# Attention jobs of a routed transformer layer: a result copy split by PSUM bank, an earlier reciprocal, and a register bound for the last stores

## The chip, the core and the metric

One NeuronCore of a Trainium2 chip. Its engines run side by side, each through its own queue, and meet only at semaphores: TensorE (PE in the profile; PEld is its weight loads), VectorE (DVE), ScalarE (ACT), GpSimd (POOL) and SyncE (SP, which issues DMAs). The metric is the device time of one execution in microseconds; lower is better.

## The reference

A gated cross-attention block and then a routed feed-forward block, float32 throughout. Two batches of 512 tokens of width 256, a context of 1024 keys, 16 heads of 64, 8 experts:

```python
# attention: q from the normalised x, k and v from the context, masked softmax
qh = heads_split(q @ Wq); kh = heads_split(k @ Wk); vh = heads_split(v @ Wv)
dots = jnp.einsum('bhid,bhjd->bhij', qh, kh) * scale
dots = jnp.where(mask[:, None, :, :], mask_value, dots)
out = einsum('bhij,bhjd->bhid', softmax(dots), vh) ... @ Wo + bo
...
# experts: each token takes the one expert with the largest gate
idx = jnp.argmax(softmax(xf @ Wg + bg), axis=-1)
h = gelu(xf @ W1[e] + b1[e]); y = h @ W2[e] + b2[e]; out = y[idx]
...
x = x + tanh(g_xattn) * attention(layernorm(x), ctx, ctx, mask)
x = x + tanh(g_ffn) * experts(layernorm(x))
```

With the inputs given, the mask leaves a window of 160 keys per batch, so the kernel takes its windowed path (`rest(False)` on all engines).

## The kernel before, in words

The order on each engine is written out by hand; semaphores tie the engines together, and nothing reorders the work afterwards. One batch of attention is `attend_window(b, ...)`, which exists once for each engine. It runs over 8 **jobs** (`JOBS`), each with two **units** (u = 2·job and 2·job + 1). A unit is one pair of heads for two tiles of 128 query rows, so it has four score blocks of 128 × 160. A unit goes through the engines so:

- PE, `scores(u)` (L1751): eight matmul records into `s_bank[u % 2]`.
- DVE, `window_max(b, u)` (L1307): for each tile, for each head, one custom instruction that scales, masks and takes a running minimum (of the negated scores). Four instructions per unit; "a pair of minima" is the two heads of one tile. `negm_ready` counts them.
- ACT, `window_exp` (L827): four exponentials per unit with their row sums, after two minima each. `probs_ready` counts units.
- DVE, `window_sum(b, u)` (L1318): the reciprocal of the row sums, into `r_col`.
- POOL, `normalise_window` (L645, L647): multiplies the unit's probabilities by the reciprocal, first the wide part (128 of the 160 keys), then the left-over 32 keys, into `left_probs`. `pn_ready` counts both.
- PE, `transposes(job)`: four transposes for the job's first unit, four for its second (L1768, into `t_bank`), and two **left transposes** (L1779) of the left-over keys. The left transposes write the upper half of PSUM bank 7, which is also the right half of `o_bank` (`o_bank[:, 1]`); its lower half holds one half of the result of the job before.
- DVE and ACT copy the transposes out of PSUM: `job_pT_rest` (L1328, a wide one of 512 columns and a left one of 256) and `job_pT_wide` (L836).
- PE, `values(job)` (L1790 left keys, L1797 wide keys), into both halves of `o_bank`.
- DVE, `job_o(b, job)` (L1333): copies the job's result out of `o_bank` to `oT`.

In the loop of job j, PE stands at scores of the next job, values of the job before, transposes of this one. In the same loop DVE does: minima of unit 2j+2 (four), reciprocal of unit 2j+1, minima of unit 2j+3 (four), copy of the result of job j−1, reciprocal of unit 2j+2, the two copies of this job's transposes, and then what hangs on `also(job)`: in the second batch, after jobs 4, 5 and 6, the normalisation of one chunk of 128 sorted rows for the experts (`norm_chunk`, L1241). POOL in the second batch also sends scatter DMAs after units 1, 3 and 5 (`sort_first_batch`, L609).

What PE waits for in `transposes(job)`: the left transposes wait for `first.o_dve`, that is for the whole copy of the result of job j−1. `values(job)` waits for the same count.

After both batches come output projections, routing, and the experts, in two rounds of eight chunks (L2000, L2011, L2022 on PE). DVE adds each chunk's result into its rows (`take_y`, L1256), and POOL sends them to their places in the output by an indirect DMA, `put_out(g, p)` (L624), 16 in all. Each has a bound on the row index, `bounds_check=T - 1`, given as a number; in the built program a register move stands ahead of each of these DMAs and carries the wait for `y_taken`. Ahead of the last of them POOL loads a flag (`over_any`, L704).

Of the kernel before, what the change touches and what calls it, by code (L numbers as in the profile page):

```python
# [97 lines left out]
def flamingo_kernel(nc, x, ctx_in, mask, g_xattn, g_ffn, wq, wk, wv, wo, bo, wg, bg, w1, b1, w2, b2, out):  # L98
# [13 lines left out]
    T = B * N  # L112
# [24 lines left out]
    with ExitStack() as stack:  # L137
# [191 lines left out]
        empty_ready = sem("empty_ready")  # L329
        s_out = sem("s_out")  # L330
        left_zero = sem("left_zero")

        head_rows = [slice(r * DH, (r + 1) * DH) for r in range(2)]

# [224 lines left out]
        def _(pool):  # L559
# [58 lines left out]
                    .then_inc(experts[g].b2_added, 1)  # L618

            out_rows = out.rearrange("b n d -> (b n) d")  # L620

            def put_out(g, p):
                pool.wait_ge(experts[g].y_taken, p + 1)
                nc.gpsimd.indirect_dma_start(out=out_rows, in_=srow[g][:, p, 0:D], in_offset=None,  # L624
                                             out_offset=bass.IndirectOffsetOnAxis(
                                                 ap=srow[g][:, p, TOKEN:RW].bitcast(I32), axis=0),
                                             bounds_check=T - 1, oob_is_err=False).then_inc(s_out, 16)

            def normalise(S, g, keys, also):
                for u in range(PER):  # L630
# [46 lines left out]
            def rest(later_too):  # L677

                if later_too:
                    pool.wait_ge(visits_listed, 1)  # L680
                for b in range(B):
                    if later_too:
                        normalise(first, b * PER, CK, nothing if b == 0 else sort_first_batch)
                    else:
                        normalise_window(b, nothing if b == 0 else sort_first_batch)
                    if later_too:
                        later_visits(b)
                    if b == 0:
                        add_bo()
                        pool.wait_ge(s_b2, 16)  # L690
                        nc.gpsimd.tensor_scalar(b2_sb[:], b2_sb[:], gate[:, 1:2], None, ALU.mult).then_inc(b2_ready, 1)

                for e in range(E):
                    add_b2(0, e, e)
                for r in range(1, len(ROUTED)):
                    pool.wait_ge(place_ready, r + 1)
                    for q in range(QT // 2):
                        scatter(r, q)
                for e in range(E):
                    put_out(0, e)  # L700
                for e in range(E - 1):
                    put_out(1, e)
                pool.wait_ge(over_ready, 1)
                any_over = pool.value_load(over_any[0:1, 0:1], min_val=0, max_val=1)  # L704
                put_out(1, E - 1)
                with pool.If(any_over > 0):
                    pool.wait_ge(over_listed, 1)
                    used = pool.value_load(over_used[0:1, 0:1], min_val=0, max_val=NV)
                    for k in range(NV):
                        with pool.If(used > k):  # L710
                            pool.reg_mov(chunk_expert, pool.value_load(over_code[0:1, k:k + 1], min_val=0, max_val=E - 1))
                            e = pool.snap(chunk_expert, min_val=0, max_val=E - 1)
                            pool.wait_ge(experts[2].sxn_ready, k + 1)
                            nc.gpsimd.tensor_tensor(srow[2][:, k, 0:D], srow[2][:, k, 0:D],
                                                    b2_sb[:, bass.ds(e, 1), :].rearrange("p e d -> p (e d)"), ALU.add)\
                                .then_inc(experts[2].b2_added, 1)
                            put_out(2, k)
                            pool.wait_ge(s_out, 16 * (B * E + k + 1))
                        with pool.Else():
                            pool.nop()  # L720
                with pool.Else():
                    pool.nop()
# [303 lines left out]
        def _(dve):  # L1026
# [266 lines left out]
                dve.wait_ge(S.o_ready, g + (u + 1))  # L1293
                nc.vector.tensor_copy(*o_dst(slot, u)).then_inc(S.o_dve, 1)

            def window_max(b, u):

                m, j = unit_of(u)
                if u >= PB:

                    dve.wait_ge(first.ptrans_ready, 3 * (b * JOBS + (u - PB) // 2) + 3)
                dve.wait_ge(first.scores_ready, b * PER + (u + 1))
                for i in range(2):
                    q = 2 * j + i
                    for h in range(2):

# [23 lines left out]
            def job_o(b, job):  # L1330
                quad, j = job // 2, job % 2
                dve.wait_ge(first.o_ready, b * JOBS + job + 1)
                nc.vector.tensor_copy(oT[:, b, 2 * quad:2 * quad + 2, j * HALF:(j + 1) * HALF],  # L1333
                                      o_bank[:, :, 0:HALF]).then_inc(first.o_dve, 1)

            def attend_window(b, w, fill, also):

# [22 lines left out]
                nc.vector.tensor_copy(*left_v_dst(3)).then_inc(first.v_dve, 1)  # L1360
                for job in range(JOBS):
                    if job + 1 < JOBS:
                        window_max(b, 2 * job + 2)
                    if job >= 1:
                        window_sum(b, 2 * job + 1)
                    if job + 1 < JOBS:
                        window_max(b, 2 * job + 3)
                    else:
                        fill(0)
# [213 lines left out]
        def _(pe):  # L1583
# [155 lines left out]
            def attend_window(b, fill, also):  # L1739
# [16 lines left out]
                def transposes(job):  # L1756
# [13 lines left out]
                        last.then_inc(first.ptrans_ready, 1)  # L1770
                    if job >= 1:

                        pe.wait_ge(first.o_dve, b * JOBS + job)
                    else:
                        pe.wait_ge(first.v_act, b * 2 + 2)
                        pe.wait_ge(first.v_dve, b * 2 + 2)
# [431 lines left out]
```

## Time and profile before

| | |
|---|---|
| median of 3 runs | 203.22 us (203.05 to 204.3) |
| the profiled execution, its own time | 204.05 us |
| its span | 202.2 us |
| PE busy | 191.9 us (95%) |
| DVE busy | 123.4 us (61%) |
| ACT busy | 106.4 us (53%) |
| POOL busy | 89.7 us (44%) |
| mean granted TensorE clock | 0.988 of full speed |

The span is what the profiler saw from the first instruction to the last; the execution's own time has 1.85 us more around it. The shares are means over stages that differ much: the attention jobs of the two batches lie at 38 to 76 us and at 112 to 146 us, the experts' second round and the last stores at 178 us to the end. The end of a matmul record is modelled by the profiler, so PE can look busy while its queue waits; the weight loads (PEld) show where it stood.

### The profile page before, as it was taken

The page shows a single profiled execution, that of the slowest core. Times are in us where ns is not written, and L with a number is a line of the kernel's source. Part 1 is how long each engine was busy: PE and PEld are TensorE (multiplying, and loading weights), DVE is VectorE, ACT ScalarE, POOL GpSimd, SP SyncE. Part 2 cuts the span into 40 slices and gives each one's busy share as a digit, 9 for nine tenths or more (in the row PEclk, how much of TensorE's full clock was granted, in tenths as well). Part 3 has the DMA queues.
Part 4 walks back from the last instruction along what each step waited for, and adds up shares of the span by engine and source line. Part 5 has one row for each costly group of instructions (what it writes and reads, how often), then busy time and mean ns, then how long its engine had stood idle before and what let it go on. Part 6 is the DMA issues. An engine that isn't in the chain of part 4 may idle for free.

```text
span 202.2 us, 3980 instructions
## 1 busy us (share of the span) xinstructions
PE 191.9 (95%) x1252; PEld 140.7 (70%) x1252; DVE 123.4 (61%) x537; ACT 106.4 (53%) x380; POOL 89.7 (44%) x129
## 2 busy tenths in 40 slices
PE   7999999899999999999999799999999999999950
PEld 6984364667775544888876566775788889989940
DVE  2479665999986421253448999997824547265520
ACT  3243537899998112211528699998441254445510
POOL 7000004367767992000002899677920014775451
PEclk9999999999999999999999999999999999999995
DMA  5997017999999980570000110600000001353011
GB/s 146 342 367 245 0 30 231 347 275 321 300 307 252 211 293 6 159 256 0 3 2 0 45 36 29 212 3 0 0 3 2 0 0 64 112 159 107 33 40 40
DMA packets 22322, 25.16 MB, mean 124 GB/s; under 512 B 1988, under 2 KB 20878, under 8 KB 22161
## 3 DMA queue, kind: packets, MB, share of 16 engines
q1 hardware_dynamic: 19536, 21.83, 36.8%
q0 software_dynamic: 1152, 2.12, 3.1%
q10 hardware_dynamic: 1600, 0.84, 1.5%
q8 instruction: 13, 0.21, 0.5%
q14 instruction: 21, 0.16, 0.3%
HBM read 14.14 MB, written 11.68 MB: 128 GB/s over the span
## 4 chain that ended last, share of the span: by engine, by line
PE 83%; DVE 9%; issue 2%; ACT 2%; POOL 1%; POOLq 0%; DVEq 0%
PE s_bank L1711 14%; PE o_bank L1656 14%; PE s_bank L2011 7%; PE o_bank L1797 7%; PE s_bank L1751 6%; PE o_bank L2022 6%; PE t_bank L1768 6%; PE o_bank L1790 3%; DVE probs L1307 3%; PE s_bank L1590 3%; DVE pT L1328 2%; PE s_bank L1822 2%; PE s_bank L1621 2%; PE t_bank L1805 2%; PE t_bank L1682 2%
## 5 line engine op out<-in xcount | busy, mean ns | idle before, releaser
L645 POOL TENSOR_TENSOR probs<-probs,r_col 128x512 f32<-128x512 f32 x32 | 33.4, 1042 | 76.4 <-DVE r_col L1318 76.1
L827 ACT ACTIVATE probs<-probs,negm_run 128x160 f32<-128x160 f32 x128 | 53.0, 416 | 5.3 <-DVE negm_run L1307 5.2
L1307 DVE CUSTOM_DVE_ANT_0 probs<-s_bank,maskneg 128x160 f32<-128x160 f32 x128 | 33.2, 318 | 3.9 <-PE s_bank L1751 3.6
L1711 PE MATMUL s_bank<-xnT,wq_sb 128*128 128x512 f32 x64 | 28.8, 597 | 0.0
L1656 PE MATMUL o_bank<-wo_sb,oT 128*128 128x256 f32 x128 | 28.7, 380 | 0.0
L1656 PEld LDWEIGHTS o_bank<-wo_sb,oT 128*128 128x128 f32 x128 | 23.9, 190 | 3.5 <-issue 0.5
L827 ACT ACTIVATION_READ_ACCUMULATOR probs<-probs,negm_run 128x1 f32 x128 | 24.0, 187 | 0.0
L1751 PE MATMUL s_bank<-k_sb,q_sb 64*128 64x160 f32 x256 | 22.1, 310 | 0.2 <-DVE negm_run L1307 0.2
L1751 PEld LDWEIGHTS s_bank<-k_sb,q_sb 64*128 64x128 f32 x256 | 17.9, 186 | 4.3 <-issue 3.5
L1711 PEld LDWEIGHTS s_bank<-xnT,wq_sb 128*128 128x128 f32 x64 | 11.7, 190 | 13.0 <-issue 12.8
L624 POOL DMA_INDIRECT out_dram<-oT x16 | 16.0, 1002 | 9.3 <-DVE oT L1256 7.2
L1768 PE MATMUL t_bank<-ident,probs 128*128 128x128 f32 x128 | 19.1, 285 | 0.2 <-POOL probs L645 0.2
L1768 PEld LDWEIGHTS t_bank<-ident,probs 128*128 128x128 f32 x128 | 13.5, 140 | 7.8 <-issue 5.7
L1797 PE MATMUL o_bank<-pT,v_sb 128*64 128x256 f32 x128 | 17.5, 393 | 0.0
L609 POOL DMA_INDIRECT sorted_rows<-rows,place x8 | 8.1, 1006 | 21.2 <-DVE place L1198 19.8
L2011 PE MATMUL s_bank<-k_sb,q_sb 128*128 128x128 f32 x128 | 17.2, 277 | 0.2 <-ACT k_sb L925 0.2
L2011 PEld LDWEIGHTS s_bank<-k_sb,q_sb 128*128 128x128 f32 x128 | 15.7, 192 | 1.0 <-ACT k_sb L925 0.5
L2022 PE MATMUL o_bank<-oT,k_sb 128*128 128x256 f32 x64 | 16.4, 383 | 0.0
L1256 DVE SCALAR_TENSOR_TENSOR oT<-o_bank,gate,oT 128x256 f32<-128x256 f32 x16 | 7.6, 483 | 12.5 <-PE o_bank L2022 12.5
L787 ACT COPY q_sb<-s_bank 128x512 f32<-128x512 f32 x10 | 5.8, 586 | 17.2 <-PE s_bank L1711 14.7
L934 ACT ACTIVATE k_sb<-s_bank,b1T 128x128 f32<-128x128 f32 x32 | 10.0, 365 | 8.8 <-PE s_bank L2011 8.4
L1230 DVE SCALAR_TENSOR_TENSOR rows<-o_bank,gate,rows 128x256 f32<-128x256 f32 x8 | 3.9, 483 | 16.1 <-PE o_bank L1656 16.1
(169 smaller groups left out, 301.1 us busy)
## 6 DMA issues: line engine op xcount, KB each, us to landing
sorted_rows<-empty_row SPq DMA_DIRECT2D x8, 1040.0 KB, 15.2
oT<-in_L_ffn_W_dram SPq DMA_DIRECT2D x1, 2048.0 KB, 19.2
q_sb<-in_L_ffn_W_dram SPq DMA_DIRECT2D x1, 2048.0 KB, 8.4
oT<-sorted_rows SPq DMA_DIRECT2D x1, 1040.0 KB, 5.0
oT<-sorted_rows SPq DMA_DIRECT2D x8, 130.0 KB, 2.3
wq_sb<-in_L_xattn_Wq_dram SPq DMA_DIRECT2D x2, 512.0 KB, 8.3
mask_sb<-in_mask_BxSxS_bk_dram SPq DMA_DIRECT2D x2, 512.0 KB, 9.1
wv_sb<-in_L_xattn_Wv_dram SPq DMA_DIRECT2D x1, 1024.0 KB, 10.8
```

The source lines that it names most:

```text
L624: nc.gpsimd.indirect_dma_start(out=out_rows, in_=srow[g][:, p, 0:D], in_offset=None, out_offset=bass.IndirectOffsetOnAxis(ap=srow[g][:, p, ...
L645: nc.gpsimd.tensor_tensor(window_wide(u), window_wide(u), r.rearrange("p i h -> p (i h)") .unsqueeze(2).broadcast_to([P, 4, WIDE]), ALU.mu ...
L827: last = nc.scalar.activation(window_part(u, i, h), window_part(u, i, h), ACT.Exp, bias=negm_run[at], scale=-1.0, accum_out=l_run[at])
L934: last = nc.scalar.activation(hT[:, p % 2, at], hT_bank(p)[:, at], ACT.Gelu, bias=bias(ic))
L1307: nc.vector.tensor_tensor_reduce(window_part(u, i, h), s_bank[u % 2][:, h, i * CK:i * CK + WK], maskneg[:, q, 0:WK], -SCALE, LARGEST, ALU. ...
L1656: last = nc.tensor.matmul(bank[6 + tt % 2][:, 0:D], oT[:, b, m, q * P:(q + 1) * P], wo_sb[:, m, :], start=(m == 0), stop=(m == M - 1))
L1711: last = nc.tensor.matmul(bank[m % 4], wq_sb[:, c, m * P:(m + 1) * P], xnT[:, c, b * N:(b + 1) * N], start=(c == 0), stop=(c == DC - 1))
L1751: last = nc.tensor.matmul(s_bank[u % 2][:, h, i * CK:i * CK + WK], q_sb[head_rows[h], b, m, q * P:(q + 1) * P], k_sb[head_rows[h], m, 0:WK ...
L1768: last = nc.tensor.transpose(bank[4 + a][:, h * HALF + i * P:h * HALF + (i + 1) * P], window_wide(u)[:, 2 * i + h, :], ident[:])
L1797: last = nc.tensor.matmul(o_bank[head_rows[h], a, 0:HALF], v_sb[:, 0, at * DH:(at + 1) * DH], wide_pT[:, a, h, :], start=False, stop=True)
L2011: last = nc.tensor.matmul(hT_bank(e)[:, ic * P:(ic + 1) * P], w1_sb[:, e, c, ic * P:(ic + 1) * P], sxT[:, e % 2, c * P:(c + 1) * P], start ...
L2022: last = nc.tensor.matmul(bank[6 + p % 2][:, 0:D], hT[:, p % 2, ic * P:(ic + 1) * P], weights(ic), start=(ic == 0), stop=(ic == IC - 1))
```

## The change

Four edits:

1. `job_o` copies the result by banks: two copies of 256 columns in place of one of 512, the right half (bank 7) first. The right half has a semaphore of its own, `o_right`; the second copy increments `o_dve`. The left transposes of the next job wait for `o_right` alone. `values` still waits for `o_dve`.
2. In DVE's loop the reciprocal of unit 2j+1 moves ahead of the second pair of minima of unit 2j+2. It stood behind it.
3. The bound of the output DMAs sits in a register that is written once at the start; the DMA itself now carries the wait for `y_taken`.
4. POOL loads the flag `over_any` after the fourth store of the second round. It was loaded after the seventh.

```diff
+        o_right = sem("o_right")
...
+            last_row = pool.alloc_register("pool_last_row")
+            pool.reg_mov(last_row, T - 1)
 
             def put_out(g, p):
                 pool.wait_ge(experts[g].y_taken, p + 1)
...
-                                             bounds_check=T - 1, oob_is_err=False).then_inc(s_out, 16)
+                                             bounds_check=last_row, oob_is_err=False).then_inc(s_out, 16)
...
-                for e in range(E - 1):
+                for e in range(E // 2):
                     put_out(1, e)
                 pool.wait_ge(over_ready, 1)
                 any_over = pool.value_load(over_any[0:1, 0:1], min_val=0, max_val=1)
-                put_out(1, E - 1)
+                for e in range(E // 2, E):
+                    put_out(1, e)
...
-            def window_max(b, u):
+            def window_max(b, u, tiles=(0, 1)):
 
                 m, j = unit_of(u)
-                if u >= PB:
-
-                    dve.wait_ge(first.ptrans_ready, 3 * (b * JOBS + (u - PB) // 2) + 3)
-                dve.wait_ge(first.scores_ready, b * PER + (u + 1))
-                for i in range(2):
+                if tiles[0] == 0:
+                    if u >= PB:
+
+                        dve.wait_ge(first.ptrans_ready, 3 * (b * JOBS + (u - PB) // 2) + 3)
+                    dve.wait_ge(first.scores_ready, b * PER + (u + 1))
+                for i in tiles:
...
                 dve.wait_ge(first.o_ready, b * JOBS + job + 1)
-                nc.vector.tensor_copy(oT[:, b, 2 * quad:2 * quad + 2, j * HALF:(j + 1) * HALF],
-                                      o_bank[:, :, 0:HALF]).then_inc(first.o_dve, 1)
+                for a, taken in ((1, o_right), (0, first.o_dve)):
+                    nc.vector.tensor_copy(oT[:, b, 2 * quad + a, j * HALF:(j + 1) * HALF],
+                                          o_bank[:, a, 0:HALF]).then_inc(taken, 1)
...
                     if job + 1 < JOBS:
-                        window_max(b, 2 * job + 2)
+                        window_max(b, 2 * job + 2, (0,))
                     if job >= 1:
                         window_sum(b, 2 * job + 1)
                     if job + 1 < JOBS:
+                        window_max(b, 2 * job + 2, (1,))
                         window_max(b, 2 * job + 3)
...
                     if job >= 1:
 
-                        pe.wait_ge(first.o_dve, b * JOBS + job)
+                        pe.wait_ge(o_right, b * JOBS + job)
```

How the rows stand on DVE in the loop of job 2, at the reciprocal. Before (each ISA pair is one minimum and the read of its result; the reciprocal is that of unit 5, between the minima of units 6 and 7):

```order
L1307 ISA probs,negm_run<-s_bank,maskneg 128x160 [waits scores_ready_first,ptrans_ready_first]
L1307 ISA negm_run 128x1
L1307 ISA probs,negm_run<-s_bank,maskneg 128x160
L1307 ISA negm_run 128x1
L1307 ISA probs,negm_run<-s_bank,maskneg 128x160
L1307 ISA negm_run 128x1
L1307 ISA probs,negm_run<-s_bank,maskneg 128x160
L1307 ISA negm_run 128x1
L1318 RECIPROCAL r_col<-l_run 128x4 [waits pn_ready_first,probs_ready_first]
L1307 ISA probs,negm_run<-s_bank,maskneg 128x160 [waits scores_ready_first,ptrans_ready_first]
```

Now:

```order
L1312 ISA probs,negm_run<-s_bank,maskneg 128x160 [waits scores_ready_first,ptrans_ready_first]
L1312 ISA negm_run 128x1
L1312 ISA probs,negm_run<-s_bank,maskneg 128x160
L1312 ISA negm_run 128x1
L1323 RECIPROCAL r_col<-l_run 128x4 [waits pn_ready_first,probs_ready_first]
L1312 ISA probs,negm_run<-s_bank,maskneg 128x160
L1312 ISA negm_run 128x1
L1312 ISA probs,negm_run<-s_bank,maskneg 128x160
L1312 ISA negm_run 128x1
L1312 ISA probs,negm_run<-s_bank,maskneg 128x160 [waits scores_ready_first,ptrans_ready_first]
```

The reciprocal stands two minima earlier, with the same waits; the third and fourth minimum are now behind those waits.

DVE again, the end of the same loop. Before:

```order
L1307 ISA negm_run 128x1
L1333 COPY oT<-o_bank 128x2x256 [waits o_ready_first]
L1318 RECIPROCAL r_col<-l_run 128x4 [waits pn_ready_first,probs_ready_first]
L1328 COPY pT<-t_bank 128x512 [waits o_ready_first,ptrans_ready_first]
L1328 COPY pT<-o_bank 128x256 [waits o_ready_first,ptrans_ready_first]
```

Now:

```order
L1312 ISA negm_run 128x1
L1339 COPY oT<-o_bank 128x256 [waits o_ready_first]
L1339 COPY oT<-o_bank 128x256
L1323 RECIPROCAL r_col<-l_run 128x4 [waits pn_ready_first,probs_ready_first]
L1333 COPY pT<-t_bank 128x512 [waits o_ready_first,ptrans_ready_first]
L1333 COPY pT<-o_bank 128x256 [waits o_ready_first,ptrans_ready_first]
```

One copy of two banks has become two copies of one bank. The rest keeps its order.

POOL, the stores at the end of the program (register moves are not listed). Before:

```order
L624 DMA out_dram<-oT 1024x256 [waits y_taken_first] x8
L624 DMA out_dram<-oT 1024x256 [waits y_taken_second] x7
L704 TENSOR_LOAD over_any [waits over_ready]
L704 ISA x2
L624 DMA out_dram<-oT 1024x256 [waits y_taken_second]
```

Now:

```order
L627 DMA out_dram<-oT 1024x256 [waits y_taken_first] x8
L627 DMA out_dram<-oT 1024x256 [waits y_taken_second] x4
L707 TENSOR_LOAD over_any [waits over_ready]
L707 ISA x2
L627 DMA out_dram<-oT 1024x256 [waits y_taken_second] x4
```

The load of the flag stands three stores earlier. PE's and ACT's queues hold the same instructions in the same order as before; on PE only the semaphore of the left transposes differs.

## Rows read from the trace of the kernel before

**Rows 1.** The chain of waits from 44 to 64 us, its shares by line.

```profile
by line: PE t_bank L1768 28.9%; PE s_bank L1751 27.1%; PE o_bank L1797 25.4%; PE o_bank L1790 10.8%; PE o_bank L1779 5.5%; PE s_bank L1711 4.3%
```

**Rows 2.** Timeline of weight loads: start us, us, engine, line, instruction, idle before.

```profile
49.63 0.42 PEld L1768 LDWEIGHTS t_bank<-ident,probs 128*128 128x128 f32 x4 [0.39 <-issue]
50.20 0.42 PEld L1768 LDWEIGHTS t_bank<-ident,probs 128*128 128x128 f32 x4
50.63 0.20 PEld L1779 LDWEIGHTS o_bank<-ident,pT 128*128 128x128 f32 x2
51.00 1.12 PEld L1751 LDWEIGHTS s_bank<-k_sb,q_sb 64*128 64x128 f32 x16 [0.17 <-issue]
55.11 1.12 PEld L1751 LDWEIGHTS s_bank<-k_sb,q_sb 64*128 64x128 f32 x16 [0.17 <-issue]
...
68.41 0.85 PEld L1768 LDWEIGHTS t_bank<-ident,probs 128*128 128x128 f32 x8 [0.39 <-issue]
69.27 0.21 PEld L1779 LDWEIGHTS o_bank<-ident,pT 128*128 128x128 f32 x2
```

**Rows 3.** Timeline of POOL, first batch and second batch.

```profile
49.10 1.04 POOL L645 TENSOR_TENSOR probs<-probs,r_col 128x512 f32<-128x512 f32 x1 [1.06 <-DVE r_col L1318]
...
120.51 0.41 POOL L647 TENSOR_TENSOR pT<-probs,r_col 128x128 f32<-128x128 f32 x1
121.03 1.04 POOL L645 TENSOR_TENSOR probs<-probs,r_col 128x512 f32<-128x512 f32 x1
```

**Rows 4.** Timeline of DVE, one loop in the first batch.

```profile
47.87 0.32 DVE L1307 CUSTOM_DVE_ANT_0 probs<-s_bank,maskneg 128x160 f32<-128x160 f32 x1 [0.40 <-PE s_bank L1751]
...
48.85 0.17 DVE L1318 RECIPROCAL r_col<-l_run 128x4 f32<-128x4 f32 x1
...
49.89 0.69 DVE L1333 COPY oT<-o_bank 128x512 f32<-128x512 f32 x1
...
50.49 0.17 DVE L1318 RECIPROCAL r_col<-l_run 128x4 f32<-128x4 f32 x1
```

**Rows 5.** Timeline of ACT, in job 1 and in a later job.

```profile
40.09 0.19 ACT L827 ACTIVATION_READ_ACCUMULATOR probs<-probs,negm_run 128x1 f32 x1
...
51.70 0.19 ACT L827 ACTIVATION_READ_ACCUMULATOR probs<-probs,negm_run 128x1 f32 x1
...
52.58 0.43 ACT L827 ACTIVATE probs<-probs,negm_run 128x160 f32<-128x160 f32 x1 [0.23 <-DVE negm_run L1307]
```

**Rows 6.** Timeline of the second batch, late jobs: DVE, and one weight load.

```profile
131.30 0.42 DVE L1328 COPY pT<-o_bank 128x256 f32<-128x256 f32 x1
131.63 0.44 DVE L1241 TENSOR_SCALAR wk_sb<-oT 128x256 f32<-128x256 f32 x1
132.12 0.32 DVE L1307 CUSTOM_DVE_ANT_0 probs<-s_bank,maskneg 128x160 f32<-128x160 f32 x1
...
139.98 0.30 PEld L1790 LDWEIGHTS o_bank<-pT,v_sb 64*128 64x128 f32 x4 [0.36 <-DVE pT L1328]
```

**Rows 7.** Timeline of DVE and POOL, a scatter's release and the last two stores.

```profile
165.48 0.17 DVE L1198 CAST place<-place_f 128x2 int32<-128x2 f32 x1
165.92 1.01 POOL L609 DMA_INDIRECT sorted_rows<-rows,place  x1 [17.71 <-DVE place L1198]
167.24 0.96 POOL L609 DMA_INDIRECT sorted_rows<-rows,place  x1 [0.30 <-issue]
...
194.25 0.48 DVE L1256 SCALAR_TENSOR_TENSOR oT<-o_bank,gate,oT 128x256 f32<-128x256 f32 x1 [1.27 <-PE o_bank L2022]
195.23 0.48 DVE L1256 SCALAR_TENSOR_TENSOR oT<-o_bank,gate,oT 128x256 f32<-128x256 f32 x1 [0.50 <-PE o_bank L2022]
195.52 0.98 POOL L624 DMA_INDIRECT out_dram<-oT  x1 [0.77 <-DVE oT L1256]
196.81 0.99 POOL L624 DMA_INDIRECT out_dram<-oT  x1 [0.30 <-issue]
```

## The prediction, made before the changed kernel was run

> **What bounds the kernel now.** I read the chain of waits first. Between 44 and 64 us, five jobs of the first batch, it lies on PE alone [rows 1]. That looks like an engine at its limit, but the end of a matmul record is modelled, so I went on to the weight loads, which show where PE's queue really stood. One job lasts 4.11 us, from the scores at 51.00 to those at 55.11 [rows 2]. In such a job the four transposes of the first unit load from 49.63, those of the second only from 50.20, after 0.15 us of nothing (49.63 + 0.42 = 50.05), and the left transposes at 50.63: 1.00 us after the first. In job 6, where projections stand between the jobs and everything has long been ready, the same ten transposes run through: 68.41 to 69.27 is 0.86 us [rows 2]. So each tight job holds 0.14 us in which PE waits, and 3.97 us are its own work.
>
> Who makes it wait? For the second unit's transposes it is POOL. Its wide multiplication runs from 49.10 to 50.14, and the load at 50.20 follows [rows 3]. POOL itself waited 1.06 us for DVE's reciprocal, which starts at 48.85, behind four minima that began at 47.87 [rows 4]; those waited for PE's scores. This is a ring: scores, four minima, reciprocal, POOL, transposes, scores. A second ring ends at the same moment: the copy of the result ends at 49.89 + 0.69 = 50.58 [rows 4], and the left transposes that wait for it load at 50.63. Taking away one of them alone would leave most of the 0.14 us. The change takes both.
>
> At the end of the program the bound is PE, then DVE, then POOL's stores. The last results are taken by 194.73 and 195.71 (starts 194.25 and 195.23 plus 0.48), and the last two stores start at 195.52 and 196.81 [rows 7].
>
> **The reciprocal earlier.** Four minima take 48.85 - 47.87 = 0.98 us, two take 0.49. The reciprocal starts 0.49 us earlier, POOL ends at 49.65 in place of 50.14, and the second unit's transposes could load at their natural 50.06. That leaves 0.4 us to spare. What is queued behind the reciprocal's wait now are the third and fourth minimum and, through them, ACT. The wait is for ACT's row sums of the unit before: their last read ends at 51.70 + 0.19 = 51.89 [rows 5], while the reciprocal would stand at 51.97 + 0.49 = 52.46. In a tight job it costs nothing. In job 1 it does: the sums end at 40.28 [rows 5] and the reciprocal would stand at about 40.15, so DVE waits some 0.15 to 0.2 us, once in each batch. Job 1 is not a tight one, and the result's copy, which is now shorter, makes up for it. I take nothing for job 1 (bounds: 0.03 gained, 0.1 lost).
>
> **The copy by banks.** A copy of 512 columns holds DVE 0.60 us (49.89 to the reciprocal at 50.49 [rows 4]), one of 256 columns 0.33 us (131.30 to 131.63 [rows 6]). So two of them take 0.66 us: 0.06 us more a job. The lower bound is nothing more; the upper is two full durations of 0.42, 0.24 us more. I take 0.06, which is read from a copy out of the same bank. The right half is ready at 49.89 + 0.42 = 50.31 in place of 50.58; the left transposes' natural place is 49.63 + 0.86 = 50.49. So this wait goes too, with 0.13 us to spare. The second copy has `values` of the next job as its waiter, over 1 us later on PE, so it costs nothing there.
>
> The Trainium skill, in VectorE: DVE Perf Modes, section on the TRN2 errata, speaks against the split: it gives a copy from PSUM to SBUF a fixed 120 cycles beside one cycle for each element. By it, as an estimate at 0.96 GHz, the second copy costs 0.125 us a job, twice the difference of the rows, and the second batch below would gain about 0.2 us less (0.065 three times).
>
> **What is late next.** PE's own 3.97 us. DVE's loop without an expert chunk is shorter: with a chunk it has 0.14 us to spare at 4.11 (the chunk starts at 131.63, holds DVE 0.44 - 0.09 = 0.35, and the next minimum comes at 132.12 [rows 6]), so 3.97 us with a chunk and 3.62 us without, and 4.03 and 3.68 after the split. ACT is idle 0.23 us a job [rows 5], so it needs 3.88.
>
> **First batch.** Five jobs have the wait (their transposes start at 45.52, 49.63, 53.74, 57.84 and 61.95): 5 x 0.14 = 0.70 us. Behind them PE runs projections without a break, so the gain is kept.
>
> **Second batch.** Five jobs again show the gap, but other engines stand close. In job 2 POOL, which also sends scatters here, is nearly full: unit 4's left part ends at 120.92 and unit 5 starts at 121.03 [rows 3]. It can start 0.1 us earlier at most: 0.09 us gained. Job 3 gains the full 0.14. From then on DVE decides, since the next loops carry the chunks: 4.11 - 4.03 = 0.08 us for each of two, and the last DVE stretch, up to the load at 139.98 that waits for the left copy [rows 6], is 0.06 us longer for the split. Sum: 0.09 + 0.14 + 0.16 - 0.06 = 0.33 us. The copy of the last job ends up to 0.06 us later with the first projection behind it; I take off 0.03. So 0.30 us. With the upper bound of the split (0.24 us) it would be 0.23 - 0.20 - 0.24, about 0.2 us lost.
>
> **The stores.** When a store has to wait for its result it starts 195.52 - 194.73 = 0.79 us after the result is taken; between lies the register move that carries the wait. The scatters carry their wait themselves: the place is there at 165.65, and the scatter starts at 165.92, 0.27 us later [rows 7]. The difference is 0.52 us. Back to back the distance is the same with and without the move (0.30 us idle between two scatters and between the last two stores [rows 7]), so nothing is gained where POOL is busy anyway. At the end: the last store but one starts at 194.73 + 0.28 = 195.01 in place of 195.52; the last follows 0.98 + 0.30 later, at 196.29, and its own result is ready by 195.71 + 0.28 = 195.99. So the end comes 0.52 us earlier; I write 0.5. The lower bound is 0, if the bound's register, which no scatter has, is what takes the time; below nothing there is no reason, since an instruction goes. The flag's load moves to where POOL idles 1 us between stores; the last two stores already stand at the back-to-back distance with it between them, so moving it gives nothing.
>
> **The sum.** 0.70 + 0.30 + 0.5 = 1.5 us. The profiled execution took 204.05 us, with a span of 202.2; it becomes 202.55, or 0.73% less. On the median of 203.22 us that is 201.7 us.
>
> **Rivals.**
> - The stores gain nothing, because reading the bound from a register is what takes the time. For it: no row shows a POOL DMA with a register that was not just written. Against: the move is the one thing that the scatter lacks and that also holds the wait. 203.2 - 1.0 = 202.2 us. Chance 0.15.
> - The loop gains nothing: PE's pieces need the 4.11 us in this order, and the 0.14 us appear again as a drain elsewhere, or DVE's dearer copy (0.24 us) takes them. Against it stand the 0.86 us of job 6. 203.2 - 0.5 = 202.7 us. Chance 0.10.
> - Slower: the reciprocal now blocks the minima. The ring is reciprocal, third and fourth minimum, ACT's six exponentials after them, row sums, the next such reciprocal. It decides as soon as ACT's sums come more than 0.57 us later than now relative to the minima (51.89 against 52.46). If the 0.17 us of job 1 came in each of the 12 later jobs: 2.0 us lost, 0.5 gained, 204.7 us. Against it: ACT has 0.23 us idle in a job. Chance 0.03.
> - More than I forecast: the 0.17 us of idle ahead of each job's scores [rows 2] is not the change of shape that it seems to be, but one more wait that goes. 10 x 0.17 us more: 200.0 us. It is there at the same length wherever scores follow left transposes, even where nothing is late. Chance 0.06.
> - The change does not do what it says, and all stays at 203.2 us. The queues show that it is built as written. Chance 0.02.
>
> **How the numbers follow.** The forecast has 0.64. Its own range is 201.2 to 202.3: the second batch between -0.2 and +0.4, the runs themselves spread by some tenths. With the first two rivals the range reaches to 203.0, and to 200.9 below for the larger gain. A measurement of this kernel can tell about 1% from no change, 2.0 us. Under 201.2 us lie the fourth rival and the lower end of the forecast: 0.15. Over 205.2 us lies hardly even the slower rival: 0.03. The rest, 0.82, is within 1%.
>
> **What the profile after would show.** Right: the distance from scores to scores 3.97 us in the first batch; second-unit transposes loading without a gap behind the first; POOL starting the odd unit about 0.75 us after the first minimum in place of 1.23; in the second batch 4.03 us where chunks are; the last store but one 0.28 us after its result. Wrong: a scores distance still at 4.11; a DVE wait on ACT at the reciprocal in every job; two result copies that hold DVE over 0.75 us together; a store 0.8 us after its result with no move ahead of it. What would make the whole wrong is a wait on PE that the modelled ends hide, since then the 0.14 us are not there to be had.

## The result, and the profile after

The changed kernel takes 202.31 us (median of 12 runs, 201.52 to 202.91) beside 203.66 us (median of 12 runs, 202.51 to 204.3) for the kernel before on the same chip. The ratio is 0.994, with a 95% interval of 0.9924 to 0.9956: 0.9 to 1.5 us were gained. (The forecast stood on the median of 3 runs on record then, 203.22 us.) The profiled execution took 201.97 us, with a span of 200.2 us, beside 204.05 and 202.2.

Timeline of the weight loads of the changed kernel, one loop of the first batch; it answers to [rows 2]:

```profile
46.31 1.12 PEld L1758 LDWEIGHTS s_bank<-k_sb,q_sb 64*128 64x128 f32 x16 [0.17 <-issue]
47.37 0.33 PEld L1797 LDWEIGHTS o_bank<-pT,v_sb 64*128 64x128 f32 x4
48.03 0.63 PEld L1804 LDWEIGHTS o_bank<-pT,v_sb 128*64 128x64 f32 x8 [0.33 <-issue]
49.05 0.86 PEld L1775 LDWEIGHTS t_bank<-ident,probs 128*128 128x128 f32 x8 [0.39 <-issue]
49.88 0.25 PEld L1786 LDWEIGHTS o_bank<-ident,pT 128*128 128x128 f32 x2
50.29 1.12 PEld L1758 LDWEIGHTS s_bank<-k_sb,q_sb 64*128 64x128 f32 x16 [0.17 <-issue]
```

The eight wide transposes are now one row: nothing stands between the first unit's and the second's. The left ones load 0.83 us after the first wide one, in place of 1.00. From scores to scores it is 50.29 - 46.31 = 3.98 us, where [rows 2] has 4.11.

POOL in the same loop answers to [rows 3], and DVE (the reads of the minima's accumulators left out) to [rows 4]:

```profile
48.03 1.04 POOL L648 TENSOR_TENSOR probs<-probs,r_col 128x512 f32<-128x512 f32 x1 [0.38 <-DVE r_col L1323]
49.03 0.40 POOL L650 TENSOR_TENSOR pT<-probs,r_col 128x128 f32<-128x128 f32 x1
```

```profile
47.29 0.32 DVE L1312 CUSTOM_DVE_ANT_0 probs<-s_bank,maskneg 128x160 f32<-128x160 f32 x1 [0.21 <-PE s_bank L1758]
...
47.78 0.17 DVE L1323 RECIPROCAL r_col<-l_run 128x4 f32<-128x4 f32 x1
...
49.31 0.75 DVE L1339 COPY oT<-o_bank 128x256 f32<-128x256 f32 x2
49.98 0.17 DVE L1323 RECIPROCAL r_col<-l_run 128x4 f32<-128x4 f32 x1
```

The reciprocal stands 0.49 us behind the first minimum and POOL starts 0.74 us behind it (48.03 - 47.29), in place of 1.23. The two copies hold DVE 49.98 - 49.31 = 0.67 us, where the one held it 0.60 [rows 4]; in the loop ahead of this one it was 0.66.

In the second batch the end of job 6 answers to the last line of [rows 6]. Weight loads, with the output projection (L1663) that closes the stretch:

```profile
138.51 0.30 PEld L1797 LDWEIGHTS o_bank<-pT,v_sb 64*128 64x128 f32 x4 [0.66 <-DVE pT L1333]
...
144.88 6.77 PEld L1663 LDWEIGHTS o_bank<-wo_sb,oT 128*128 128x128 f32 x32
```

The wait there has grown from 0.36 to 0.66 us. At the end of the program, the timeline of DVE and POOL answers to [rows 7]:

```profile
192.82 0.48 DVE L1260 SCALAR_TENSOR_TENSOR oT<-o_bank,gate,oT 128x256 f32<-128x256 f32 x1 [1.27 <-PE o_bank L2029]
193.58 0.98 POOL L627 DMA_INDIRECT out_dram<-oT  x1 [0.77 <-DVE oT L1260]
193.80 0.48 DVE L1260 SCALAR_TENSOR_TENSOR oT<-o_bank,gate,oT 128x256 f32<-128x256 f32 x1 [0.50 <-PE o_bank L2029]
194.87 0.99 POOL L627 DMA_INDIRECT out_dram<-oT  x1 [0.30 <-issue]
```

The last store but one starts 193.58 - 193.30 = 0.28 us after its result is taken, in place of 0.79, and the last one 1.29 us later, as before. The trace of before has 16 register moves of 29 ns at the stores' line (L624) in POOL's queue; the trace of after has none at L627.

**Where the time went.** A span alone does not tell it well: it also holds the start (the first query projection loads at 13.59 us before, at 13.16 after) and the landing of the last store. So I cut the program at weight loads and the last store, which are there in every kernel. Each column is the distance between two marks: job 1's scores to job 2's; job 2's to job 6's (four loops); to the second batch's first scores (the fifth loop and the projections); to job 2's scores there; four loops; to the first output projection (L1656 before, L1663 after); to the start of the last store. All in us, worked out from the starts in the timelines of one execution each.

```
kernel          1-2    2-6   to b2   to 2   2-6  to proj  to store    sum  against before
before         5.03  16.42   46.51  13.10  16.43  11.05    50.51   159.05
after          5.00  15.91   46.36  13.08  15.91  11.28    49.99   157.53   -1.52
loop_only      5.00  15.91   46.37  13.07  15.91  11.29    50.50   158.05   -1.00
stores_only    5.04  16.42   46.50  13.11  16.42  11.05    49.99   158.53   -0.52
copy_only      5.03  16.42   46.50  13.10  16.42  11.17    50.50   159.14   +0.09
recip_only     5.20  16.42   46.50  13.27  16.42  11.05    50.51   159.37   +0.32
split_no_early 5.26  16.68   46.62  13.33  16.69  11.22    49.99   159.79   +0.74
recip_first    5.48  16.67   46.57  13.55  16.67  11.50    49.99   160.43   +1.38
move_then_wait 5.01  15.90   46.37  13.08  15.91  11.29    49.99   157.55   -1.50
old_flag       5.01  15.91   46.37  13.08  15.91  11.28    49.99   157.55   -1.50
```

Where two kernels do the same thing in a stretch, they agree within 0.02 us. The change gained 0.51 + 0.15 us in the first batch's loops, 0.52 in the second's, lost 0.23 behind them, gained 0.52 at the stores and 0.05 in small ends: 1.52 us.

### The profile page after: what moved, and what is told of

Same layout as the page of the kernel before. It is cut to its first block, busy times and chain, and to the rows that moved or that the text cites. A ratio compares the mean times of both kernels' runs of the same rounds, so it can differ in the third digit from the quotient of the medians.

```text
span 200.2 us, 3981 instructions
## 1 busy us (share of the span) xinstructions
PE 189.0 (94%) x1252; PEld 139.3 (70%) x1252; DVE 124.0 (62%) x553; ACT 106.2 (53%) x380; POOL 90.5 (45%) x129
## 4 chain that ended last, share of the span: by engine, by line
PE 81%; DVE 9%; DMA 3%; ACT 2%; issue 2%; POOLq 1%; ACTq 0%; POOL 0%; DVEq 0%
PE s_bank L1718 14%; PE o_bank L1663 14%; PE s_bank L2018 7%; PE o_bank L1804 7%; PE o_bank L2029 7%; PE s_bank L1758 6%; PE t_bank L1775 6%; PE o_bank L1797 4%; DVE probs L1312 3%; DMA wk_sb<-in_L_xattn_Wk_dram 3%; PE s_bank L1829 2%; DVE pT L1333 2%; PE s_bank L1628 2%; PE t_bank L1812 2%; PE t_bank L1689 2%
## 5 line engine op out<-in xcount | busy, mean ns | idle before, releaser
L1663 PE MATMUL o_bank<-wo_sb,oT 128*128 128x256 f32 x128 | 28.8, 380 | 0.0
L1663 PEld LDWEIGHTS o_bank<-wo_sb,oT 128*128 128x128 f32 x128 | 23.9, 190 | 3.5 <-issue 0.5
L627 POOL DMA_INDIRECT out_dram<-oT x16 | 17.0, 1064 | 7.8 <-DVE oT L1260 6.0
L1775 PE MATMUL t_bank<-ident,probs 128*128 128x128 f32 x128 | 17.7, 280 | 0.2 <-POOL probs L648 0.2
L1339 DVE COPY oT<-o_bank 128x256 f32<-128x256 f32 x32 | 12.0, 417 | 3.6 <-PE o_bank L1804 3.6
```

Source lines behind the costliest of these rows:

```text
L1339: nc.vector.tensor_copy(oT[:, b, 2 * quad + a, j * HALF:(j + 1) * HALF], o_bank[:, a, 0:HALF]).then_inc(taken, 1)
L1663: last = nc.tensor.matmul(bank[6 + tt % 2][:, 0:D], oT[:, b, m, q * P:(q + 1) * P], wo_sb[:, m, :], start=(m == 0), stop=(m == M - 1))
L1775: last = nc.tensor.transpose(bank[4 + a][:, h * HALF + i * P:h * HALF + (i + 1) * P], window_wide(u)[:, 2 * i + h, :], ident[:])
```

## The experiments

### The two halves of the change

`loop_only` has the split copy and the moved reciprocal, the stores and the flag as before. `stores_only` is the reverse.

```
loop_only:   - bounds_check=last_row    + bounds_check=T - 1     (flag after the seventh store)
stores_only: - for a, taken in (...)    + one copy of o_bank[:, :, 0:HALF], L1768 waits for o_dve
             - window_max(.., (0,)); window_sum; window_max(.., (1,))   + window_max; window_sum
```

> The loop's two edits (the split copy with its early release, the reciprocal between the minima), with the stores' bound an immediate and the flag where it was. My theory, two rings in the loop and a DMA that waited behind a register move: the scores' loads of the first batch's tight jobs stand 3.98 us apart, the last store but one begins 0.79 us after its result, and the time is 1.0 us (0.5%) under the kernel before, ratio 0.995 (0.993 to 0.998). Rival, all of the gain came from the stores: the ratio is 1.000. Rival, the register also speeds the loop: the loop is 4.1 us here.

> The two edits of the stores (bound in a register, flag read after the fourth store), the attention loop as before. My theory: the loop stays at 4.11 us, no MOVE rows of the POOL queue between the stores, the last store but one begins 0.28 us after its result, ratio 0.9975 (0.996 to 0.999), 0.5 us. Rival, the stores gain nothing since the DMA is bound by something else: ratio 1.000 with the 0.79 us still there.

Measured: `loop_only` 202.74 us beside 203.51, ratio 0.995 (0.9929 to 0.9971); its loops are 3.98 us, and it is 1.00 us shorter in the table. `stores_only` 203.08 us, ratio 0.999 (0.9967 to 1.0014): too little for the timing alone, but in the table only the last column moves, by 0.52 us. The halves do not touch each other: 1.00 + 0.52 = 1.52. The rivals, all from the stores, nothing from the stores, and a register that speeds the loop, are out. The stores of `loop_only` look as before the change. Its chain of waits (start, us, what; POOLq is POOL's queue, where the register moves stand):

```profile
191.68 0.49 DVE oT L1257
192.17 0.02 issue
192.20 0.03 POOLq L625
192.22 0.73 issue
192.96 0.98 POOL out_dram L625
```

The result is taken at 191.68 + 0.49 = 192.17, the register move follows at 192.20 and the store 0.76 us behind the move.

### The loop's two edits, each alone

```
copy_only:   reciprocal back behind the unit's second tile; split copy and o_right kept
recip_only:  one copy, left transposes wait for o_dve; reciprocal between the tiles kept
(both with the stores and the flag of before)
```

> Only the split copy and its early release; the reciprocal stands behind the second minima as before, the stores as before. My theory of two rings: the ring through POOL (reciprocal, two normalising steps, the second unit's transposes) still holds the loop near 4.1 us, so the left transposes stop waiting but the transposes of the second unit go on waiting; the loop is 4.05 to 4.15 us and the time within 0.2 us of before (ratio 0.999 to 1.001). Rival, one ring through the result copy alone: the loop is 3.98 us and the ratio 0.995.

> Only the reciprocal between the minima; the result is copied by one instruction and the left transposes wait for all of it, the stores as before. My theory: the copy of the result now ends last ahead of the left transposes, with what remains of the 0.14 us split between the rings; the loop is 4.00 to 4.08 us, ratio 0.997 to 1.000. Rival, POOL's ring was the only one: loop 3.98 us, ratio 0.995, and the split copy is worth nothing.

Measured: `copy_only` 203.55 us beside 203.51, ratio 1.0002 (0.9977 to 1.0028), loops of 4.105 us. `recip_only` 204.01 us, ratio 1.002 (1.0004 to 1.0036), loops of 4.105 us as well. So neither edit gains anything alone and the two together gain 0.13 us a loop; the one-ring rivals, which asked for 3.98 us, are out. What holds each is in its weight loads. `copy_only`, with the wide multiplication of POOL for the second unit:

```profile
44.83 0.98 PEld L1771 LDWEIGHTS t_bank<-ident,probs 128*128 128x128 f32 x8 [0.39 <-issue]
45.81 0.22 PEld L1782 LDWEIGHTS o_bank<-ident,pT 128*128 128x128 f32 x2
...
44.30 1.04 POOL L646 TENSOR_TENSOR probs<-probs,r_col 128x512 f32<-128x512 f32 x1 [0.77 <-DVE r_col L1320]
```

`recip_only`:

```profile
45.71 0.86 PEld L1771 LDWEIGHTS t_bank<-ident,probs 128*128 128x128 f32 x8 [0.38 <-issue]
46.72 0.20 PEld L1782 LDWEIGHTS o_bank<-ident,pT 128*128 128x128 f32 x2
```

In the first the eight wide transposes are stretched to 0.98 us, since the second four wait for POOL, which is done at 44.30 + 1.04 = 45.34; the first four, 0.42 us long, have loaded by 45.25. In the second they run through in 0.86, and the left ones come 0.15 us behind them, held by the copy. I had expected some of the 0.14 us to be left over in `recip_only` (4.00 to 4.08); there is none: the two rings are equally long, within what these traces tell apart. And `recip_only` is not merely worth nothing: it loses 0.17 us in job 1 of each batch. Its DVE there:

```profile
39.93 0.32 DVE L1309 CUSTOM_DVE_ANT_0 probs<-s_bank,maskneg 128x160 f32<-128x160 f32 x1
...
40.33 0.18 DVE L1320 RECIPROCAL r_col<-l_run 128x4 f32<-128x4 f32 x1
...
40.12 0.19 ACT L828 ACTIVATION_READ_ACCUMULATOR probs<-probs,negm_run 128x1 f32 x1
```

The second minimum starts at 39.93 and its accumulator read at 40.17, where the reciprocal starts in a later loop (in the rows of the changed kernel above, 0.49 us behind the first minimum). Here it starts at 40.33, when ACT's last read of the sums ends (40.12 + 0.19 = 40.31). The copy of the result comes that much later, and the whole of it releases the left transposes, which wait ("0.21 <-DVE oT L1335" at 42.61). In the changed kernel the two copies start at 41.42, the first half is done at about 41.84 (0.42 us for 256 columns), and the left transposes load at 41.92 without a wait.

### The split without its early release

```
- for a, taken in ((1, o_right), (0, first.o_dve)):
+ for a, taken in ((0, o_right), (1, first.o_dve)):
- pe.wait_ge(o_right, b * JOBS + job)
+ pe.wait_ge(first.o_dve, b * JOBS + job)
```

> The changed kernel with the copy still split but its halves in the order left, right and the left transposes released by the last of the two, so the split costs its extra instruction and releases nothing early. My theory: the left transposes wait for the end of both copies, as for the one copy before but 0.06 us later; the loop is 4.02 to 4.12 us instead of 3.98, and the time 0.3 to 0.8 us over the changed kernel. Rival, the release is worth nothing once the reciprocal has moved: 3.98 us, the same time as the changed kernel.

Measured: 204.83 us beside 203.54, ratio 1.0059 (1.0039 to 1.0079). Loops of 4.17 us, 0.19 over the changed kernel, 0.06 to 0.07 over the kernel before; in the table 159.79 - 157.53 = 2.3 us over the changed kernel. I had given 0.3 to 0.8 us and had the loops too short (4.02 to 4.12). What follows is simple: the ring through the result copy is 4.105 us with one copy (`recip_only`) and 4.17 with two, so the second instruction costs 0.06 us, and all of the split's value is in releasing the right half first.

### The reciprocal ahead of all minima

```
+ if job >= 1: window_sum(b, 2 * job + 1)       (ahead of the unit's first tile)
  window_max(b, 2 * job + 2); window_max(b, 2 * job + 3)
```

> The changed kernel with the reciprocal ahead of all four minima instead of between the first two and the last two. My theory: VectorE waits there for ScalarE's sums, since they end only shortly before; that wait (0.05 to 0.3 us) lies where VectorE otherwise waits for the scores or has slack in the first batch, so the first batch's loop stays 3.98 to 4.0 us; in the second batch, where VectorE has a loop of 4.03 us of its own, the time grows by 0.1 to 0.5 us. Rival, the reciprocal's wait blocks the minima in every job: over 0.15 us in each of 12 jobs, 2 us or more over the changed kernel.

Measured: 205.13 us beside 203.54, ratio 1.0078 (1.0051 to 1.0104). My theory fell: loops of 4.17 us in both batches, and 0.48 us lost in job 1 of each. DVE:

```profile
47.27 0.18 DVE L1323 RECIPROCAL r_col<-l_run 128x4 f32<-128x4 f32 x1 [0.34 <-ACT probs L831]
47.38 0.33 DVE L1312 CUSTOM_DVE_ANT_0 probs<-s_bank,maskneg 128x160 f32<-128x160 f32 x1
...
51.43 0.18 DVE L1323 RECIPROCAL r_col<-l_run 128x4 f32<-128x4 f32 x1 [0.35 <-ACT probs L831]
```

ACT, between these two reciprocals:

```profile
47.99 0.43 ACT L831 ACTIVATE probs<-probs,negm_run 128x160 f32<-128x160 f32 x1 [0.29 <-DVE negm_run L1312]
...
51.22 0.18 ACT L831 ACTIVATION_READ_ACCUMULATOR probs<-probs,negm_run 128x1 f32 x1
```

DVE waits for ACT in every loop. The reciprocal waits for the sums, the minima for the reciprocal, ACT's eight exponentials for the minima, and the next sums for these: 51.43 - 47.27 = 4.16 us is a ring of its own. It is a longer form of the slower rival's ring in the prediction, brought about by one place in DVE's order. With the reciprocal between the tiles, the first two minima and the two exponentials that hang on them do not wait for the sums, and this ring is shorter than the loop. The time over the changed kernel is 160.43 - 157.53 = 2.9 us, close to what the rival in this experiment gave.

### Register and flag

```
move_then_wait:   def put_out(g, p):
                +     pool.reg_mov(last_row, T - 1)
                      pool.wait_ge(experts[g].y_taken, p + 1)
old_flag:       flag read after the seventh store of the second group, as before the change
```

> The changed kernel with the bound's register written again before each store, ahead of the store's wait, so that a register is still moved but nothing stands between the wait and the store. My theory, the 0.51 us of a store before came from the move that stood between wait and store: the store begins 0.28 us after its result as in the changed kernel and the time is the changed kernel's. Rival, any move beside a store costs: 0.79 us and 0.5 us more time.

> The changed kernel with the flag read after the seventh store, as before the change, the bound still in the register. My theory, as in the prediction: moving the flag gains nothing by itself; POOL's read of 0.36 us now stands in front of the last store, whose turn comes 0.30 us after the seventh, so the last store starts up to 0.4 us later and the time is 0 to 0.3 us over the changed kernel. Rival, the read costs what it takes: 0.4 to 0.5 us over the changed kernel.

Measured: `move_then_wait` 202.5 us beside 203.54, ratio 0.9956 (0.9941 to 0.9972). The 16 moves are back, but ahead of the wait. Its chain of waits:

```profile
192.30 0.98 POOL out_dram L628
193.28 0.54 issue
193.82 0.03 POOLq L626
193.85 0.20 issue
194.05 0.81 POOL out_dram L628
```

The result of the seventh store is taken at 193.29 + 0.48 = 193.77 and its store starts at 194.05, 0.28 us later. (The move at 193.82 is already the eighth store's: it is the last of 16, and it runs as soon as the seventh store has been handed over.) So a register that is written again costs nothing; a move that stands between wait and store costs 0.51 us. The move itself lasts 0.03 us; what the rest of that time is, no row shows. `old_flag` 202.63 us, ratio 0.9954 (0.9938 to 0.997), last column 49.99: the read of the flag costs nothing where it was; the 0 to 0.3 us that I had left for it are 0. Its chain:

```profile
192.93 0.39 POOLq L707
193.32 0.20 POOL out_dram L627
...
194.45 0.99 POOL out_dram L627
```

The queue reads the flag from 192.93 to 193.32. The seventh store starts at 193.16 in the timeline, and the last one 1.29 us behind it, at 194.45, the same distance as without the read between them.

### A version beyond the change

With loops at 3.98 us and no wait of PE for another engine in them, the weak place is what comes ahead. In the changed kernel, PE's weight loads at the start of job 1 wait twice:

```profile
37.34 1.18 PEld L1758 LDWEIGHTS s_bank<-k_sb,q_sb 64*128 64x128 f32 x16 [0.17 <-DVE negm_run L1312]
39.38 0.30 PEld L1797 LDWEIGHTS o_bank<-pT,v_sb 64*128 64x128 f32 x4 [0.87 <-DVE pT L1333]
40.01 0.20 PEld L1804 LDWEIGHTS o_bank<-pT,v_sb 128*64 128x64 f32 x4 [0.33 <-issue]
40.52 0.20 PEld L1804 LDWEIGHTS o_bank<-pT,v_sb 128*64 128x64 f32 x4 [0.30 <-ACT pT L840]
```

Six microseconds earlier DVE stands idle:

```profile
33.91 0.18 DVE L1323 RECIPROCAL r_col<-l_run 128x4 f32<-128x4 f32 x1 [1.46 <-ACT probs L831]
```

So the third unit's scores, minima and exponentials were moved ahead of the second and third value projection (`third_ahead`: first batch; `third_ahead2`: both).

```
PE   project_v(0); + scores(2); project_v(1); project_v(2); job 0: - scores(2)  scores(3)
DVE  window_sum(b, 0); + window_max(b, 2); window_sum(b, 1) ...   job 0: - window_max(b, 2)
ACT  copy of v 0; + window_exp(b, 2); left copies; job 0: window_exp(b, 3)
```

> A version beyond the change, on top of the changed kernel: in the first batch the scores of the third unit are issued ahead of the second and third value projection, VectorE takes their minima while it would wait 1.46 us for ScalarE, and ScalarE takes their exponentials ahead of the copies of the left values. My theory: TensorE's two waits at the start of job 1 (0.87 us for VectorE's copy, 0.30 us for ScalarE's copy) shrink, and the stretch from the first scores to the third job's scores, 13.48 us in the changed kernel, becomes 0.6 to 1.2 us shorter; ratio to the kernel before 0.988 to 0.992. Rival, the waits only move to the transposes of job 0, since POOL's normalising is what comes last: no more than 0.2 us over the changed kernel's 0.994.

> The same in both batches. My theory: a second 0.6 to 1.2 us in the second batch, where TensorE has the same two waits (0.87 and 0.30 us) and two more of 0.24 and 0.41 us for the minima; ratio to the kernel before 0.983 to 0.988. Rival, in the second batch the minima of the third unit delay VectorE's routing work and with it POOL's scatters, which ends up ahead of the expert stage: no gain over the first batch alone.

Measured: `third_ahead` 202.02 us beside 203.87, ratio 0.990 (0.9876 to 0.9923). The loads of its job 1:

```profile
38.67 1.12 PEld L1764 LDWEIGHTS s_bank<-k_sb,q_sb 64*128 64x128 f32 x16 [0.17 <-DVE negm_run L1314]
39.83 0.30 PEld L1803 LDWEIGHTS o_bank<-pT,v_sb 64*128 64x128 f32 x4
40.47 0.63 PEld L1810 LDWEIGHTS o_bank<-pT,v_sb 128*64 128x64 f32 x8 [0.33 <-issue]
...
42.72 1.12 PEld L1764 LDWEIGHTS s_bank<-k_sb,q_sb 64*128 64x128 f32 x16 [0.17 <-issue]
```

Both waits are gone, and job 1 takes 4.05 us in place of 5.00. Part of it is given back ahead: from the first scores to job 1's it is 8.88 us in place of 8.48 (the load of the third unit's scores waits 0.76 us for the minima). The stretch to job 2's scores is 12.93 us in place of 13.48, 0.55 shorter, just under the 0.6 to 1.2 expected. Its other stretches are the changed kernel's within 0.02 us. It was timed against the kernel before only, at another time than the changed kernel; against that one the 0.55 us of the trace and the two ratios, 0.990 and 0.994, point the same way, but the intervals leave no gap between them (one ends at 0.9923, the other begins at 0.9924).

`third_ahead2` 202.57 us, ratio 0.9937 (0.9913 to 0.996): the second batch takes the gain back. From its first scores to job 2's it is 118.06 - 104.30 = 13.76 us, where the changed kernel has 13.08. POOL and DVE tell why:

```profile
110.51 0.17 DVE L1325 RECIPROCAL r_col<-l_run 128x4 f32<-128x4 f32 x1
...
112.34 1.18 POOL L610 DMA_INDIRECT sorted_rows<-rows,place  x1 [0.18 <-issue]
113.82 0.96 POOL L610 DMA_INDIRECT sorted_rows<-rows,place  x1 [0.30 <-issue]
114.80 1.06 POOL L648 TENSOR_TENSOR probs<-probs,r_col 128x512 f32<-128x512 f32 x1
```

Two scatters stand ahead of the third unit's normalising in POOL's queue, in both kernels. Counted from the batch's first scores, that normalising starts at 10.50 us here and at 9.79 in the changed kernel (114.80 - 104.30 and 114.40 - 104.61). The 0.71 us arise one step earlier, on DVE: the four minima of the third unit (0.98 us) and the value copy behind them stand ahead of the routing work and of the second unit's reciprocal, which starts 6.21 us after the first scores in place of 5.48 (110.51 - 104.30 and 110.09 - 104.61). The first scatter is late by the same 0.73 us, and so PE waits 0.87 us for POOL at 117.26. This is the rival's mechanism; what it had wrong is the place, since the loss shows in job 1 of this batch and not at the experts, and it is the size of the first batch's gain.

## Why the prediction was right

The forecast was 201.7 us in a range of 200.9 to 203.0, with a chance of 0.82 for no change that this measurement can tell. The median is 202.31 us, the gain 0.6%. Of the 0.6 us between forecast and median, 0.44 lie in the kernel before, which is at 203.66 us over 12 runs and not at 203.22, and 0.15 in the gain. On the terms:

- **First batch, 5 x 0.14 = 0.70 us.** 0.51 for four loops, 0.15 for the fifth: 0.66. The loop was forecast at 3.97 and is 3.98 us. That both edits are needed ("taking away one of them alone would leave most of the 0.14 us") is shown by `copy_only` and `recip_only`, which have 4.105 us; it leaves all of it.
- **The reciprocal.** Its wait in job 1 is there, 0.16 us in `recip_only`. That the shorter release makes up for it was right as well: job 1 went from 5.03 to 5.00 us, and without the release it is 5.20.
- **The split.** 0.06 us a job was forecast and 0.06 measured, by DVE's rows and by the loops of `recip_only` and `split_no_early` (4.105 and 4.17). The Trainium skill, in VectorE: DVE Perf Modes, section on the TRN2 errata, with its fixed 120 cycles for each such copy, gives an estimate of 0.125 us; here the rows and the loops say half of that, and the measurement decides.
- **Second batch, 0.30 us.** 0.31 measured, from other terms than mine. The step that failed is "from then on DVE decides, since the next loops carry the chunks", and with it POOL's limit in job 2: all four loops are 3.98 us and gain their full 0.13 (0.52). POOL had 0.16 us to give and not 0.1: I took the end of one row (120.92) for the moment at which the next can start, but units 4 and 5 start 119.71 - 118.35 = 1.36 us apart after the change, where it was 121.03 - 119.51 = 1.52. DVE's own loops with a chunk are 4.05 and 4.03 us, as forecast: its first minima of jobs 4, 5 and 6 start at 126.62, 130.67 and 134.70. But the first of them had waited 0.18 us for the scores, so the delay of 0.05 to 0.07 us a loop against PE's 3.98 did not hold PE at once. It was paid in one piece at the load at 138.51, where PE, now early, waits 0.66 us. From the last scores to that load it is 138.51 - 133.60 = 4.91 us, beside 139.98 - 135.25 = 4.73: 0.12 us for the two late loops and 0.06 for the split. `copy_only`, which has the split but no late loops, bears this out: there it is 139.32 - 134.53 = 4.79, 0.06 more than before. The first output projection comes 0.05 us later again, where 0.03 was forecast. So the sum came out in part because the same 0.12 us of DVE stands in it, only at another place, and in part by luck: the small errors of the other terms cancel.
- **The stores, 0.52 us.** 0.52 in `stores_only` and in the changed kernel. The reason, the place of the move between wait and store, is shown by `move_then_wait`. The flag's move gives nothing: `old_flag`.
- **The sum.** 1.5 us forecast, 1.52 in the table. The medians say 1.35 us, and the interval of the ratio reaches from 0.9 to 1.5, so the timing alone does not tell the terms apart; the table does.

Of the rivals, the stores that gain nothing and the loop that gains nothing are out by the two halves. The larger gain, from the 0.17 us ahead of the scores, is out: they are unchanged in the loop at 46.31 and 50.29 in which nothing else waits. The slower one did not come, but `recip_first` shows that such a ring is real. The margin, 0.57 us by the rows of before, is 0.45 us in the changed kernel with its shorter loop (ACT's last read ends at 51.12 + 0.19 = 51.31, the reciprocal starts at 51.76). Moving the reciprocal 0.49 us further is more than that, and once it waits, all four minima and all eight exponentials wait behind it: 4.17 us a loop is the result.

## What to carry to other kernels

Where two waits in a loop end at the same moment, each alone is worth nothing, or less than nothing: count the rings, and judge their edits together. An instruction that takes a result early should stand as far forward as its own inputs allow with margin, and not one step further; the price of that step is a new ring. A gain in a loop is passed on only as far as the next engine's slack lasts, so read its first wait behind the loop before and after.

## What the runs showed of the hardware

- A register move between a semaphore wait and POOL's indirect DMA costs 0.51 us (0.79 against 0.28 us from result to store); ahead of the wait, the same move costs nothing.
- The read of a flag of 0.39 us in POOL's queue between two indirect DMAs that follow each other without a wait is free: the second starts 1.29 us after the first with it and without it.
- Where two kernels do the same thing, whole stretches of 16 to 50 us repeat within 0.02 us from one profiled execution to the next, while the medians carry tenths. What varies is the start (first query projection between 12.20 and 14.10 us in these traces) and the landing of the last store (4.75 to 5.55 us from its start to the end of the span). A gain of 0.5 us, which the timing of `stores_only` could not tell from none, is plain in the table.
